# A router's rank products: two choices' masks summed on VectorE, one set of products on TensorE

## What the reference computes

```
logits = jnp.einsum('bsd,de->bse', x, Wg) + bg
topk_vals, topk_idx = jax.lax.top_k(logits, TOP_K)      # TOP_K = 2
topk_w = jax.nn.softmax(topk_vals, axis=-1)
h = jax.nn.relu(jnp.einsum('bsd,edf->bsef', x, W1) + b1)
eo = jnp.einsum('bsef,efd->bsed', h, W2) + b2
sel = jnp.take_along_axis(eo, topk_idx[..., None], axis=2)
mixed = jnp.sum(sel * topk_w[..., None], axis=2)
```

## Time and profile before

| | |
|---|---|
| Median of 3 runs | 2422.21 us |
| Lowest and highest | 2421.08 and 2422.56 us |
| Span of the profiled execution, first to last instruction | 2425.2 us |
| First stage, to the meeting of the engines | about 1845 us |
| PE busy in the span | 2186.3 us (90%) |
| DVE busy | 2038.4 us (84%) |
| POOL busy | 1827.8 us (75%) |
| ACT busy | 1506.5 us (62%) |
| Mean granted clock of TensorE | 0.965 of full |

### The profile page before, as it was taken

How to read it: one execution, slowest core, us unless ns; L and a number is a source line. 1 busy time by engine, 2 the same in 40 slices (tenths; PEclk the granted TensorE clock), 3 DMA queues, 4 the chain that set the end, 5 groups by cost and what they waited for, 6 DMA issues and landing times. The chain is left out here.

```text
span 2425.2 us, 47399 instructions
## 1 busy us (share of the span) xinstructions
PE 2186.3 (90%) x13721; PEld 1766.3 (73%) x13722; DVE 2038.4 (84%) x3037; ACT 1506.5 (62%) x3292; POOL 1827.8 (75%) x1093
## 2 busy tenths in 40 slices
PE   8889899998989898998989898999787999999980
PEld 5667677677777666777777776767676999999970
DVE  5999999999999999999999999999974555555558
ACT  6687877878786877878787878877741111111106
POOL 3888989889898989889888989898962434444447
PEclk9999999999999999999999999999987999999995
DMA  5041322314041323324041413223137998999978
GB/s 172 7 134 54 131 75 102 124 52 164 21 158 48 131 69 114 106 70 153 32 156 34 144 49 135 80 96 116 62 123 199 226 228 229 229 230 229 229 166 277
DMA packets 186791, 312.50 MB, mean 129 GB/s; under 512 B 18851, under 2 KB 118083, under 8 KB 186500
## 3 DMA queue, kind: packets, MB, share of 16 engines
q1 hardware_dynamic: 140932, 258.53, 33.4%
q0 software_dynamic: 25584, 34.62, 7.5%
q10 hardware_dynamic: 20112, 17.32, 2.2%
HBM read 247.09 MB, written 63.32 MB: 128 GB/s over the span
## 5 line engine op out<-in xcount | busy, mean ns | idle before, releaser
L855 POOL TENSOR_TENSOR dbu<-drive_u,b_rows 128x1024 f32<-128x1024 f32 x384 | 904.3, 2363 | 87.7 <-DVE ps_a L660 35.1
L1159 ACT ACTIVATE ps_a<-delta,a_neg 128x512 f32<-128x512 f32 x768 | 517.2, 685 | 136.9 <-DVE ss L660 120.2
L872 POOL TENSOR_TENSOR wp<-ss,rows_c 128x1024 f32<-128x1024 f32 x192 | 453.6, 2363 | 37.6 <-DVE ss L660 36.9
L1766 POOL DMA_INDIRECT acc_scratch<-ow,idx x135 | 211.2, 1564 | 309.2 <-issue 102.4
L672 DVE TENSOR_TENSOR wd<-ps_a,rows_c 128x1024 f32<-128x1024 f32 x320 | 383.3, 1198 | 0.0
L1437 PEld LDWEIGHTS ps_y<-ident,wd 128*128 128x128 f32 x2560 | 299.4, 143 | 98.7 <-issue 70.5
L1437 PE MATMUL ps_y<-ident,wd 128*128 128x128 f32 x2560 | 337.3, 277 | 12.4 <-DVE wd L672 12.4
L1804 ACT COPY e_meta<-xt 128x2 f32<-128x2 f32 x135 | 25.9, 192 | 439.0 <-PE e_ps_x L1877 294.4
L1464 PEld LDWEIGHTS ps_a<-dg,duT 128*128 128x128 f32 x2048 | 248.6, 196 | 60.6 <-issue 58.1
L1464 PE MATMUL ps_a<-dg,duT 128*128 128x128 f32 x2048 | 259.0, 281 | 31.6 <-ACT carry L1166 28.6
L1688 DVE TENSOR_SCALAR e_hT<-e_ps_h,b_turned 128x128 f32<-128x128 f32 x540 | 152.1, 344 | 144.7 <-PE e_ps_h L1886 125.2
(11 more groups left out here) (200 smaller groups left out, 3653.8 us busy)
## 6 DMA issues: line engine op xcount, KB each, us to landing
b_rows<-in_L_ffn_W_dram SPq DMA_DIRECT2D x135, 512.0 KB
rows_c<-b_scratch SPq DMA_DIRECT2D x128, 512.0 KB, 4.9
b_rows<-b_scratch SPq DMA_DIRECT2D x96, 512.0 KB, 4.1
xt<-xs_scratch SPq DMA_DIRECT2D x135, 129.0 KB
xb<-in_L_attn_x_dram SPq DMA_DIRECT2D x16, 512.0 KB, 4.0
hx<-in_L_attn_x_dram SPq DMA_DIRECT2D x16, 512.0 KB, 6.3
x_scratch<-hx SPq DMA_DIRECT2D x16, 512.0 KB, 2.9
acc_scratch<-stage SPq DMA_DIRECT2D x16, 512.0 KB, 2.9
```

Source lines behind the costliest of these rows:

```text
L855: pool.tensor_tensor(dbu[:, k % NBU], du[:, g % 2, :].unsqueeze(1).broadcast_to([P, 2, CH]), bb[:, row:row + 2, :], ALU.mult).then_inc(dbu ...
L872: pool.tensor_tensor(wp[:, s % 2], ss[:, s % 2], cc[:, rows, :], ALU.mult).then_inc(wp_done, 1)
L1159: act.activation(dst, dl[:, g, :], ACT.Exp, scale=a_neg[:, g, n:n + 1]).then_inc(exp_done, 1)
L1766: pool.indirect_dma_start(out=acc_dram, out_offset=bass.IndirectOffsetOnAxis(ap=idx[:, old, :], axis=0), in_=ow[:, old, :], in_offset=None ...
```

## The change

A new tile `both` takes the sum of the two masks, made on DVE by the unused routing step 12, which is put right after step 9 at offset 41. PE's `rank` waits for step 12 before it begins, and then runs one triangular product and 4 products with ones on `both`, instead of one such set for each choice. Waits and counts of the routing steps are renumbered (12 for each chunk).

```diff
+        both = sb("both", [P, NT, E])
...
-        ROUTE = (38, 39, 40, 40, 40, 41, 41, 41, 41, 41, 45, 45, 45, 45)
+        ROUTE = (38, 39, 40, 40, 40, 41, 41, 41, 41, 41, 45, 45, 41, 45)
+        ROUTE_ORDER = (0, 1, 2, 3, 4, 5, 6, 7, 8, 9, 12, 10, 11, 13)
...
-            return route, 11 * q + (j + 1 if j < 9 else j)
+            return route, 12 * q + {12: 10, 10: 11, 11: 12}.get(j, j + 1)
...
-                    dve.wait_ge(*routed(q, {7: 5, 8: 6, 13: 10}.get(j, j - 1)))
+                    dve.wait_ge(*routed(q, {7: 5, 8: 6, 12: 9, 10: 9, 13: 10}.get(j, j - 1)))
...
+                elif j == 12:
+                    ins = dve.tensor_tensor(both[:], sel[:, 0], sel[:, 1], ALU.add)
...
-                for j, offset in enumerate(ROUTE):
-                    q = due(at, offset, -1)
-                    if q is not None and j != 12:
+                for j in ROUTE_ORDER:
+                    q = due(at, ROUTE[j], -1)
+                    if q is not None:
                         route_step(q, j)
...
                 elif kind == "rank":
-                    pe.wait_ge(*routed(q, 3))
+                    pe.wait_ge(*routed(q, 12))
                     if q > 0:
                         pe.wait_ge(*routed(q - 1, 13))
                     pe.matmul(dst[:, 0:(NT + 1) * E], ident[:], seen[:].unsqueeze(1).broadcast_to([P, NT + 1, E]),
                               start=True, stop=False, skip_group_check=True)
-                    for k in range(2):
-                        if k == 1:
-                            pe.wait_ge(*routed(q, 9))
-                        pe.matmul(dst[:, 0:NT * E], below[:], sel[:, k].rearrange("p i e -> p (i e)"), start=False,
-                                  stop=False, skip_group_check=True)
-                        for i in range(NT):
-                            ins = pe.matmul(dst[:, (i + 1) * E:(NT + 1) * E], ones[:],
-                                            sel[:, k, i, :].unsqueeze(1).broadcast_to([P, NT - i, E]), start=False,
-                                            stop=(k == 1 and i == NT - 1), skip_group_check=True)
+                    pe.matmul(dst[:, 0:NT * E], below[:], both[:].rearrange("p i e -> p (i e)"), start=False,
+                              stop=False, skip_group_check=True)
+                    for i in range(NT):
+                        ins = pe.matmul(dst[:, (i + 1) * E:(NT + 1) * E], ones[:],
+                                        both[:, i, :].unsqueeze(1).broadcast_to([P, NT - i, E]), start=False,
+                                        stop=(i == NT - 1), skip_group_check=True)
```

## The result

| | before | after |
|---|---|---|
| Median of 13 runs each, side by side | 2422.21 us | 2428.97 us |
| Lowest and highest | 2420.4 and 2426.78 us | 2427.3 and 2431.31 us |
| Span of the profiled execution | 2425.2 us | 2426.4 us |

The ratio is 1.0027, 95% interval 1.0018 to 1.0035: the kernel became slower by 6.8 us. The forecast was 2423.2 us with 2427.5 as its upper end, so the result lies outside the range. The profiled spans differ by 1.2 us only. The two executions profiled are not equally typical: that of after has a time of its own, 2428.32 us, 1.9 above its span, while that of before had a span alone.

What follows compares the result with a forecast made beforehand. DVE was taken to set the pace around a rank, with PE's work there free except in the last chunk. Addition + 2.2 and last chunk - 1.2 gave + 1.0 us on 2422.2, so 2423.2 us; range 2419.2 to 2427.5.

Steps and rivals of the forecast that it cites:

- One addition of 128x32 float32 ... the upper one 0.30, if nothing overlaps: DVE behind step 9: the added step costs 0.20 us a chunk, 0 to 0.30; 11 chunks pay, 2.2 us.
- The step is dearer and the end gives nothing: Rival: addition costs 4.5 us, last chunk gains nothing, 2426.7 us; with one more low-clock chunk 2428.4; chance 0.03.
- PE's ten instructions for nothing: PE, 15 ranks beside scans: removing ten of 22 instructions frees 1.11 us each, 16.7 us, but gains nothing in time.
- PE's new wait: PE ahead of each rank: waiting for step 12 instead of step 3 costs nothing, PE arriving 2.0 us later.
- The last chunk: Last rank, running alone: step 10 comes 1.25 us earlier, taken as 1.2 us gain, between 0 and 2.1 us.
- Step 10 2.8 to 3.3 us behind step 9 instead of 4.53: Sign in the last chunk: this shorter distance on DVE would show the forecast gain.
- The first set did not hide anything: Last chunk before: step 9 starts during the counts' product, so the first set's ten instructions stand ahead of the second's.
- The low clock spreads: Rival: TensorE's clock falls in the gap behind the rank, about 1.7 us per hit chunk, 2428 to 2433 us; chance 0.10.
- the sign the prediction had named against itself: Prediction wrong if any odd chunk, or more than six even ones, shows DVE waiting for L1464 ahead of the rank.
- The cited rule on the clock: Trainium skill on TensorE: clock is granted by how busy PE has been, which speaks against taking work from PE.
- PE's time comes through: Rival: each rank shortens its chunk by 1.11 us, 16.7 us over 15, about 2404 us, half of it 2413; chance 0.05.
- The term for the low clock: TensorE at half clock ahead of even ranks: 1.7 us per hit chunk; two more or fewer make 3.4 us.

Runs made afterwards that it cites:

- sbuf_add_only: Kernel before plus an unused DVE addition between steps 8 and 9, of first mask and a constant tile, both in SBUF; 2431.47 us, ratio 1.0032.
- psum_add_only: Kernel before plus an unused DVE addition between steps 8 and 9, second operand the comparison in PSUM; 2422.42 us, ratio 0.9994.
- psum_same_place: Changed kernel with the addition still behind step 9, but its second operand read from PSUM; 2425.43 us, ratio 1.0009.
- psum_sum: Changed kernel with the addition's second operand read from PSUM and the addition moved between steps 8 and 9; short PE rank; 2424.10 us, ratio 0.9999.
- psum_sum_b: psum_sum run again unchanged; 2422.55 us, ratio 0.9989 to the kernel before.
- null: Kernel before, unchanged, run and profiled again; 2422.29 us, ratio 0.9998, span 2420.4 us.
- add_only: Changed kernel's routing with the addition made but its sum unused, PE's rank products as before (22 instructions); 2427.44 us, ratio 1.0014.
- after_again: Changed kernel, unchanged, run and profiled again; 2429.21 us, ratio 1.0021 to the kernel before, span 2426.3 us.

## Why the prediction was wrong

**The step that failed: "One addition of 128x32 float32 ... the upper one 0.30, if nothing overlaps".** It measured 0.63 us in each of the chunks where it is paid, three times the 0.20 taken and twice the upper bound. The order of the sequence was right (step 9 to addition 0.22 us, addition to scan without delay); the duration was not. The rows that stood in for it, L591 at 0.17 us and the masks at 0.19, each read one operand from PSUM (`ps_p`), and the addition reads both from SBUF. No other DVE instruction of the routing does. It was called nearest by operation and size, and the memory of the operands was not looked at. Nor was POOL: at step 9 it is in the middle of a 2.36 us product of SBUF tiles, in 15 chunks out of 16. `sbuf_add_only` against `psum_add_only` shows that the operand makes the difference, `psum_same_place` that with it exchanged the term is 0.22 us as meant, and the last chunk's 192 and 166 ns that POOL has to be at work for it. The Trainium skill ("SBUF — State Buffer", section "Who interferes with whom") has the rule: a DVE instruction with two inputs in SBUF contends with a GpSimd instruction that reads SBUF, the one issued second stands until the first is done, and with at most one input in SBUF, outside the modes that use both ports, there is no contention. The trace agrees where POOL was first, with 0.60 and 0.94 us that end 0.05 us behind POOL's product, 0.16 to 0.19 us with an operand in PSUM, and POOL's own product at 2364 ns in after; no row looked at here has the addition first and POOL behind it. The rule spoke against this change and was not weighed.

With the measured term in the prediction's own sum, 11 x 0.63 = 6.9 instead of 2.2 us, the forecast would have been 2427.9; without a gain at the end 2429.1, against 2428.97 measured. With the ten chunks that paid in after's profile it is 6.3 us and 2428.5. That the first comes so close is partly luck, since the medians of one kernel differ by more than that. The rival nearest to what happened was "The step is dearer and the end gives nothing", with a chance of 0.03: right in its kind, and bounded too low, at 0.30 us a chunk, to reach past the limit.

**PE's ten instructions for nothing: right.** Cover and place were as said; the idle time ahead of the transpose grew to 1.98 us, of which 1.1 was forecast, and no chunk became shorter. `psum_sum` and `psum_sum_b` against `psum_add_only`, which differ in PE's rank alone, give 0.9999 and 0.9989 against 0.9994. The list of DVE's waits that this started from was incomplete, though: its largest sum was left out, 26.9 us in 15 waits for ACT's decays (L1159). None of it lies in the 50 us behind the third rank, and it is 26.5 us in after, so nothing hung on it.

**PE's new wait: right in 14 ranks, and without a cost in the fifteenth.** PE arrives at 447.83, 1.6 us behind the end of the addition, late as that is. At the fifteenth rank it does wait for it: PE starts 0.11 us behind the end of the addition after 2.57 us idle (1.91 in before, behind step 9). DVE's step 10 still comes 6.57 us behind step 9, as at the other odd ranks (6.58 or 6.59), so nothing is lost by it.

**The last chunk: right against the profile used, not shown as a gain.** "Step 10 2.8 to 3.3 us behind step 9 instead of 4.53" measured 3.32, just past the upper end. But "The first set did not hide anything" held for that execution and not for `null`, where the first set began 0.66 us before step 9 and ran at the full clock. A single profile of a stretch that meets either clock was taken for the kernel, and it was the longest of the five with two sets.

**The low clock spreads (0.10): did not happen.** The idle time became longer than that rival assumed, 1.98 us, and the mean granted clock is 0.967 against 0.965. Long waits for the drives ahead of a rank: four in before, five in `null`, five in after. Two of after's are at odd ranks, the sign the prediction had named against itself, but two of `null`'s are as well: it was a sign of nothing, taken from one execution. The cited rule on the clock therefore changed nothing here, and the earlier trace rows don't bear it out either: PE is busy 3.40 of 3.40 us in both stretches, at 0.50 and at 1.00. **PE's time comes through (0.05): did not happen.** The term for the low clock, 3.4 us either way, was a fair size for the spread of single executions; the medians of the kernel before on the chips used here lay between 2422.21 and 2424.09 us. The range was given its width there, while the term that was off had a narrow bound.

**What stays open.** Two profiles of the kernel before differ by 4.8 us. 2.3 of it is the last chunk and 3.4 lies ahead of the first rank's step 10 (232.84 and 229.39 us), partly given back between; what makes the early part differ was not followed. What sets the clock in the last chunk is not shown either, nor why `add_only` is 1.8 us faster than `after_again`.

## What to carry to other kernels

Price an instruction that is added to VectorE by rows that agree in where the operands are, not only in operation and size, and look at what GpSimd does at that moment: with both operands in SBUF a 0.19 us addition lasted until GpSimd's product was done. With one operand from PSUM it cost 0.22 us in the same place, and nothing where its engine waits for a dependence anyway; the place alone, with both operands in SBUF, saved nothing (0.75 us). And before a gain is counted at a place whose clock can be either of two, look at a second execution.

## What the runs showed of the hardware that was not expected

- A DVE addition of 32 columns waits inside its own duration for a running POOL product, with no wait in the list of waits: 593 and 932 ns at the median against 161 with an operand in PSUM. The loss shows only as busy time, so it is found by the least and greatest duration of one instruction.
- POOL doesn't pay: its product lasts 2364 ns in after and 2363 in before.
- The clock that TensorE has for the last, lonely rank differs between executions of one kernel: 4.53 and 2.27 us from step 9 to step 10 in two of the kernel before, 2.75 and 2.12 us in two of `psum_sum`. Of nine executions with 0 to 0.12 us or 1.5 us of idle time ahead of that rank, seven had nearly all its products at half clock, three of them without the idle time.
